# The residual x1 + b3 made in the base stage of a two-layer LoRA, convolution and gated-FFN kernel, with the convolution's last loads reordered

## The reference, cut to what matters

```python
# x: (32, 64, 1024) = 2048 rows of 1024
x = x + L0_ffn(L0_cond(x, cond))     # = x1
x = x + L1_ffn(L1_cond(x1, cond))    # = x1 + silu-gated FFN of the convolved x1

# L0_cond: a 64x64 channel mix per batch (a mixture of 8), plus a bias           -> y
# L0_ffn:  y @ kernel + bias + LoRA of the group's own adapter and a shared one
# L1_cond: grouped 1-d convolution of x1 with 9 taps, plus a context and a bias   -> c
# L1_ffn:
x12 = einsum('bsk,mk->bsm', c, w12) + b12
x1_, x2_ = split(x12, 2)
return einsum('bsm,nm->bsn', silu(x1_) * x2_, w3) + b3
# and the last line of the whole: out = x1 + (... @ w3.T + b3)
```

## Time and profile before

| | us |
|---|---|
| median of 3 runs | 844.76 |
| lowest, highest | 843.33, 848.78 |
| the profiled execution | 842.09 |
| its span, first to last instruction | 840.3 |
| TensorE busy | 819.3 (98%) |
| DVE busy | 384.4 (46%) |
| ACT busy | 150.0 (18%) |
| POOL busy | 84.6 (10%) |

### The profile page before, as it was taken

How to read it: one execution, slowest core, us unless ns; L and a number is a source line. 1 busy time by engine, 2 the same in 40 slices (tenths; PEclk the granted TensorE clock), 3 DMA queues, 4 the chain that set the end, 5 groups by cost and what they waited for, 6 DMA issues and landing times.

```text
span 840.3 us, 10782 instructions
## 1 busy us (share of the span) xinstructions
PE 819.3 (98%) x4081; PEld 691.8 (82%) x4081; DVE 384.4 (46%) x456; ACT 150.0 (18%) x194; POOL 84.6 (10%) x59
## 2 busy tenths in 40 slices
PE   5998999999999999999999999999999989999998
PEld 4876888888888999888888888888888868888886
DVE  4864442414230787525343433121243975655552
ACT  3431110101000334201120112010102432111110
POOL 4440433231321000000000000000000000000000
PEclk9999999999999999999999999999999999999999
DMA  8946853643639872335353533020334244444441
GB/s 249 284 127 207 217 143 92 154 122 112 164 86 238 215 171 62 116 135 166 126 168 121 170 131 100 25 75 25 104 96 112 87 163 151 150 151 150 164 161 75
DMA packets 72873, 116.89 MB, mean 139 GB/s; under 512 B 10680, under 2 KB 50024, under 8 KB 72840
## 3 DMA queue, kind: packets, MB, share of 16 engines
q1 hardware_dynamic: 69632, 115.35, 46.4%
q10 hardware_dynamic: 3064, 0.90, 0.6%
q0 software_dynamic: 144, 0.21, 0.1%
HBM read 70.92 MB, written 44.45 MB: 137 GB/s over the span
## 4 chain that ended last, share of the span: by engine, by line
PE 89%; DVE 4%; DMA 3%; issue 1%; SPq 1%; ACTq 1%; ACT 0%; DVEq 0%
PE ps L1285 72%; PE ps L1546 17%; DVE w_t_f L1086 1%; DMA lb<-lb_c_lo 1%; DMA raw<-in_L_ffn_w 1%; DMA h_f<-h_scratch 1%; ACTq L323 1%; DVE w_t_lo L1091 1%; SPq L465 1%; DVE h_s L1133 0%; DMA gate_t<-in_L_ffn_gate 0%; PE ps L1330 0%; DVE w_n L1080 0%; DVE lb_c_lo L991 0%; DVE hs_lo L1203 0%
## 5 line engine op out<-in xcount | busy, mean ns | idle before, releaser
L1285 PE MATMUL ps<-c_hi,w_hi 128*128 128x512 f32 x512 | 199.3, 389 | 0.0
L1285 PE MATMUL ps<-c_hi,w_lo 128*128 128x512 f32 x512 | 199.2, 389 | 0.0
L1285 PE MATMUL ps<-c_lo,w_hi 128*128 128x512 f32 x512 | 199.2, 389 | 0.0
L1133 DVE SCALAR_TENSOR_TENSOR h_s<-ps,b_s,silu_s 128x512 f32<-128x512 f32 x32 | 24.0, 751 | 195.9 <-PE ps L1285 195.6
L1285 PEld LDWEIGHTS ps<-c_hi,w_hi 128*128 128x128 f32 x512 | 96.1, 188 | 20.1
L1285 PEld LDWEIGHTS ps<-c_lo,w_hi 128*128 128x128 f32 x512 | 96.1, 188 | 19.9
L1285 PEld LDWEIGHTS ps<-c_hi,w_lo 128*128 128x128 f32 x512 | 96.1, 188 | 19.8
L1285 PE MATMUL ps<-wk_hi,y_hi 128*128 128x512 f32 x256 | 80.5, 395 | 0.4 <-issue 0.4
L1285 PE MATMUL ps<-wk_lo,y_hi 128*128 128x512 f32 x256 | 79.1, 390 | 0.0
L1285 PE MATMUL ps<-wk_hi,y_lo 128*128 128x512 f32 x256 | 78.9, 389 | 0.0
L979 DVE TENSOR_TENSOR x_t<-ps,x_t 128x1024 f32<-128x1024 f32 x16 | 19.6, 1225 | 122.2 <-PE ps L1285 118.0
(11 more groups left out here) (156 smaller groups left out, 961.1 us busy)
## 6 DMA issues: line engine op xcount, KB each, us to landing
raw<-in_L_ffn_w SPq DMA_DIRECT2D x96, 128.0 KB, 3.1
x_scratch<-x_t SPq DMA_DIRECT2D x16, 516.0 KB, 2.7
x_scratch<-x_t SPq DMA_DIRECT2D x128, 64.5 KB, 2.4
x<-x_scratch SPq DMA_DIRECT2D x32, 258.0 KB, 6.1
x_in<-x_scratch SPq DMA_DIRECT2D x16, 516.0 KB, 4.1
x_in<-in_x SPq DMA_DIRECT2D x16, 512.0 KB, 4.5
h_scratch<-h_s SPq DMA_DIRECT2D x32, 256.0 KB, 2.2
r_scratch<-r_t SPq DMA_DIRECT2D x16, 512.0 KB, 2.9
```

Of the source, the lines that this page charges most:

```text
L1133: dve.scalar_tensor_tensor(out=h_s[rb][:, :], in0=bank(2 * rb + 1), scalar=b12_s[:, 1, ds(j, 1)], in1=silu_s[rb % 2][:, :], op0=ALU.add, o ...
L1285: return pe.matmul(o, l, r, start=start, stop=stop)
```

## The change

The rows of x1 are no longer stored to DRAM and loaded back. DVE makes r from the tile `x1_t` in the base stage, directly behind take_x1, into one of two buffers `r_t` that lie where raw[0] and raw[1] lie, and SP stores it behind the eight x8 stores of the tile. `b3_s` moves to raw[2]'s place and is loaded in the setup. As the buffers of w12 are now taken by r_t until the last r store, `load_w12(0)` moves behind these stores; slices 4 and 5 of the convolution are loaded ahead of that wait. The gate stage loses the residuals and is written as a loop on DVE.

```diff
-    x1_dram = nc.dram_tensor("x1_scratch", [ROWS, PH * (BLK + 1)], F32).ap()
...
-        x1_in = at("x1_in", [P, 2, HB + 1], 182.25)
-        r_t = at("r_t", [P, NL], 186.3125)
-        b3_s = at("b3_s", [P, NL], 190.3125)
+        r_t = [at(f"r_t{s}", [P, NL], 199.75 + 4 * s) for s in range(2)]
+        b3_s = at("b3_s", [P, NL], 90)
...
             load_wk(6)
             load_wk(7)
+            wait_slot(sp, raw_of(5))
+            sp.dma_start(b3_s[:, :], b3.partition_broadcast(P)).then_inc(b3_in, 16)
             sp.wait_ge(lbs_made, 2)
...
             def store_x1(t, s, made):
                 sp.wait_ge(x1_made, made)
                 sp.wait_ge(pads_made, 4)
-                sp.dma_start(x1_dram[ds(t * P, P), :], slots(x1_t[s])).then_inc(x1_stored[s], 16)
                 for n in range(2 * GRP):
                     sp.dma_start(x8_rows[n, ds(t, 1)].rearrange("a c k e -> (a c) k e"),
                                  slots(x1_t[s])[n * CG:(n + 1) * CG, :].rearrange("p (k e) -> p k e", e=BLK + 1)
                                  ).then_inc(x1_stored[s], 16)
+                sp.wait_ge(r_made, made - 2)
+                sp.dma_start(r_dram[ds(t * P, P), :], r_t[s][:, :]).then_inc(r_stored[s], 16)
...
             load_c_bias(0)
-            load_w12(0)
             sp.wait_ge(y_mm, 2 * TILES)
             sp.wait_ge(xb_made, TILES)
             for s in range(2):
-                sp.wait_ge(x1_stored[s], 144 * 2)
+                sp.wait_ge(x1_stored[s], 128 * 2)
             for t in range(4):
                 load_x8(t)
             store_x1(TILES - 2, 0, TILES + 1)
             store_x1(TILES - 1, 1, TILES + 2)
             load_c_bias(1)
             for s in range(2):
-                sp.wait_ge(x1_stored[s], 144 * TILES // 2)
-            for t in range(4, TILES):
+                sp.wait_ge(x1_stored[s], 128 * TILES // 2)
+            load_x8(4)
+            load_x8(5)
+            for s in range(2):
+                sp.wait_ge(r_stored[s], 16 * TILES // 2)
+            load_w12(0)
+            for t in range(6, TILES):
                 load_x8(t)
...
-            sp.wait_ge(conv_mm, NB)
-            sp.dma_start(b3_s[:, :], b3.partition_broadcast(P)).then_inc(b3_in, 16)
-            sp.wait_ge(c_taken, NB + 8)
-            with sp.Fori(0, 4) as j:
-                load_w12(j + 1)
-                for rb in range(RB):
-                    load_x1(j * 4 + rb)
-                    store_h(j, rb)
-                    store_r(j * 4 + rb)
-            with sp.Fori(4, NJ - 2) as j:
+            with sp.Fori(0, NJ - 2) as j:
                 load_w12(j + 1)
                 for rb in range(RB):
                     store_h(j, rb)
...
-            sp.wait_ge(r_stored, 16 * TILES)
...
-                    pool.wait_ge(x1_stored[k % 2], i * 288 + 144 * (k // 2 + 1))
+                    pool.wait_ge(x1_stored[k % 2], i * 256 + 128 * (k // 2 + 1))
+                    pool.wait_ge(r_made, i * 4 + k + 1)
...
+            def residual(t, s, free):
+                dve.wait_ge(x1_made, t + 3)
+                if free is not None:
+                    dve.wait_ge(r_stored[s], free)
+                dve.tensor_tensor(r_t[s][:, :].rearrange("p (b h q) -> p h q b", h=2, q=4), blocks(x1_t[s]),
+                                  b3_s[:, :].rearrange("p (b h q) -> p h q b", h=2, q=4), ALU.add).then_inc(r_made, 1)
+
+            dve.wait_ge(b3_in, 16)
+            for pair in range(2):
+                dve.wait_ge(lb_stored[pair], 64)
+            dve.wait_ge(lb_loaded[0], LB_FIRST[0])
+            residual(0, 0, None)
+            residual(1, 1, None)
+
             def take_group(i, k):
                 t, g = i * 4 + 2 * k, i * 2 + k
                 take_y(t + 2, 1 - k, 0)
                 take_x1(t, 0)
+                residual(t, 0, i * 32 + 16 * k)
                 take_y(t + 3, 1 - k, 1)
                 take_x1(t + 1, 1)
+                residual(t + 1, 1, i * 32 + 16 * k)
                 take_z(g + 1, 1 - k)
...
-            def gate_steps(i, with_residual):
+            def gate_steps(i):
...
-            gate_steps(0, True)
-            gate_steps(1, True)
-            gate_steps(2, False)
-            dve.wait_ge(r_stored, 16 * TILES)
+            gate_steps(0)
+            with dve.Fori(1, 3) as i:
+                gate_steps(i)
```

More of the change, by code:

```diff
@@ L262, in layered_kernel @@
         h_loaded = [sem(f"h_loaded{s}") for s in range(2)]
-        x1_loaded, r_made, r_stored = sem("x1_loaded"), sem("r_made"), sem("r_stored")
+        r_made, r_stored = sem("r_made"), [sem(f"r_stored{s}") for s in range(2)]
         w3_hi_made, w3_lo_made, w3_sum_made = sem("w3_hi_made"), sem("w3_lo_made"), sem("w3_sum_made")
@@ L519, in store_h @@
                              h_s[rb][:, :]).then_inc(h_stored[rb], 16)
-            def load_x1(t):
-                sp.wait_ge(r_made, t + 1)
-                sp.dma_start(slots(x1_in), x1_dram[ds(t * P, P), :]).then_inc(x1_loaded, 16)
-            def store_r(t):
-                sp.wait_ge(r_made, t + 2)
-                sp.dma_start(r_dram[ds(t * P, P), :], r_t[:, :]).then_inc(r_stored, 16)
-            sp.wait_ge(conv_mm, NB)
-            sp.dma_start(b3_s[:, :], b3.partition_broadcast(P)).then_inc(b3_in, 16)
-            sp.wait_ge(c_taken, NB + 8)
-            with sp.Fori(0, 4) as j:
-                load_w12(j + 1)
-                for rb in range(RB):
-                    load_x1(j * 4 + rb)
-                    store_h(j, rb)
-                    store_r(j * 4 + rb)
-            with sp.Fori(4, NJ - 2) as j:
+            with sp.Fori(0, NJ - 2) as j:
                 load_w12(j + 1)
@@ L673, in _ @@
             for t in range(TILES - 4, TILES - 2):
-                pool.wait_ge(x1_stored[t % 2], 144 * (t // 2 + 1))
+                pool.wait_ge(x1_stored[t % 2], 128 * (t // 2 + 1))
+                pool.wait_ge(r_made, t + 1)
                 pool.wait_ge(x_loaded[(t + 2) % 4], 16 * ((t + 2) // 4 + 1))
@@ L881, in _ @@
             dve.sem_inc(h_made, 4)
-            dve.sem_inc(r_made, 1)
             dve.wait_ge(consts_made, 2)
@@ L1049, in _ @@
             take_x1(12, 0)
+            residual(12, 0, 96)
             take_y(15, 1, 1)
             take_x1(13, 1)
+            residual(13, 1, 96)
             take_z(7, 1)
             take_x1(14, 0)
+            residual(14, 0, 112)
             take_x1(15, 1)
+            residual(15, 1, 112)
             def turn(n_in, s, value, half, n_free):
@@ L1137, in _ @@
             dve.wait_ge(c_lo_made, NB + 4)
-            def residual(j, rb):
-                dve.wait_ge(x1_loaded, (j * 4 + rb) * 16 + 16)
-                if not (isinstance(j, int) and j == 0 and rb == 0):
-                    dve.wait_ge(r_stored, (j * 4 + rb) * 16)
-                dve.tensor_tensor(r_t[:, :].rearrange("p (b h q) -> p h q b", h=2, q=4), blocks(x1_in),
-                                  b3_s[:, :].rearrange("p (b h q) -> p h q b", h=2, q=4), ALU.add).then_inc(r_made, 1)
-            def gate_steps(i, with_residual):
+            def gate_steps(i):
                 for k in range(2):
@@ L1150, in gate_steps @@
                     turn_w12(j + 1)
-                    if with_residual:
-                        residual(j, 0)
                     hidden(j, 1)
                     w12_lo_part(j + 1, 1 - k)
-                    if with_residual:
-                        residual(j, 1)
-                    for rb in range(2, RB):
-                        hidden(j, rb)
-                        if with_residual:
-                            residual(j, rb)
-            dve.wait_ge(b3_in, 16)
-            gate_steps(0, True)
-            gate_steps(1, True)
-            gate_steps(2, False)
-            dve.wait_ge(r_stored, 16 * TILES)
+                    hidden(j, 2)
+                    hidden(j, 3)
+            gate_steps(0)
+            with dve.Fori(1, 3) as i:
+                gate_steps(i)
             hidden(6, 0)
```

2 lines of the change are left out of this document (1 added, 1 removed).

## The result

The changed kernel took 850.22 us (median of 20 runs, 843.29 to 854.62) beside 844.94 us for the kernel before on the same chip (20 runs): ratio 1.005, 95% interval 1.0029 to 1.007. The forecast was 846.0 us with a range of 842.0 to 851.5. So the time lies in the range and within 1% of the forecast, but the forecast's +1.2 us were +5.3 us, and no step of the sum comes to that.

A forecast was written before the change was run, and what follows sets the result against it. The prediction took TensorE, busy 98% of the span, as the bound. Its terms 0 + 0 + 0.5 + 0.7 = +1.2 us on 844.76 gave 846.0 us, with an 8-in-10 range of 842.0 to 851.5.

The forecast's parts named there:

- the forecast's +1.2 us: Whole kernel: sum of 0 + 0 + 0.5 + 0.7 us, added to 844.76 to give 846.0 us.
- What bounds the kernel: From 69 to 640 us TensorE waits once, 3.8 us; only what delays TensorE counts.
- Part 1: Gate stage: residual additions, x1 loads and r stores leave a stage where TensorE never waits; worth 0.
- Part 2: Base stage: residual added behind take_x1; tightest at z_group(2), margin 0.8 us, cost 0, bounds 0 to 1.4 us.
- DVE late at z_group(2), 1.4 us at most: Rival in the base stage's first group: TensorE waits for DVE, at most 1.4 us, 847.4 us; chance 0.04.
- Wrong: a wait of TensorE at z_group(2): Sign against the forecast: TensorE waiting at z_group(2) or any later group in the base stage.
- Part 3: SP's setup queue: early b3 load delays y_bias about 4.7 us, to 52.5; cost 0.5 us, bounds 0 to 2.2.
- The +0.5 us: Setup term: y_bias' data overlapping the critical LoRA copies on the DMA engines, taken near the low end.
- Part 4: Base-to-convolution seam: w12(0) and r store ahead of x8(6) make TensorE wait 0.7 us, bounds 0 to 2.0.
- x8(4): 286.0 + 0.8 = 286.8 against 287.2, no wait: Convolution start: x8(4), 0.8 us later for the r store, still lands before TensorE needs it.
- The rival with the fallen clock: Seam: TensorE waits 2.0 us, then a slowed clock costs 1.6 more, 848.9 us; chance 0.11.
- y_bias ahead of the copies: Setup rival: y_bias goes out just before the sixteen critical copies, 2.2 us instead of 0.5, 847.7 us; chance 0.08.

The follow-up runs named there:

- after_again: The changed kernel, unchanged, run once more as yardstick for the other runs; 851.63 us, 1.0068 against the kernel before.
- b3_behind: The changed kernel with b3's load and its wait moved behind the six shared LoRA copies, ahead of the x tiles; 853.07 us, 1.0092.
- slices_first: The changed kernel with x8(6) to x8(8) loaded ahead of the wait for the r stores and of w12(0); 851.39 us, 1.0049.
- seam_alone: The changed kernel with last r store, second c_bias and w12(0) behind x8 loads at the seam, DVE order unchanged; 850.64 us, 1.007.
- y_first: The changed kernel with take_y of the second tile and take_z ahead of the residuals on DVE, all groups; 849.14 us, 1.0047.
- y_setup: The changed kernel with y_first's DVE order, b3 behind the shared copies, x tile 5 behind group 1's LoRA loads; 847.73 us, 1.0018.
- before_again: The kernel before, unchanged, one execution for a second profile; 847.92 us.
- before_add: The kernel before plus one unused DVE addition with two SBUF inputs behind take_x1(2) in the first group; 847.59 us, 1.0016.
- before_b3: The kernel before with the changed kernel's early b3 load and its wait, into a tile nobody reads; 848.43 us, 1.0029.
- all_moves: The changed kernel with y_first's DVE order, b3 behind the shared copies, x tile 5 behind group 1's LoRA loads, and a reordered seam; 845.82 us, 1.0002.
- y_seam: The changed kernel with y_first's DVE order and all_moves' seam, b3 and x tile 5 left in the changed kernel's places; 845.23 us, 0.9996.

## Why the forecast was too low

**The account that the table gives.** z_group(2): the five profiles with after's order on DVE (after, after_again, b3_behind, slices_first, seam_alone) lose 0, 4.1, 5.4, 6.2 and 6.0 us against 171.11 in the base groups, a mean of 4.3 us; the eight with another order and no added addition lose 0.0. The seam: the five with after's seam (after, after_again, b3_behind, y_first, y_setup) take 411.76 to 415.41 us for convolution and gate, mean 412.75; the four profiles with before's seam (before, before_again, before_add, before_b3) 410.10 to 412.39, mean 410.8: 2.0 us. Together 6.3 us, from single executions, beside +5.3 and +6.4 us between the medians. Setup and first group: u_lora(3) starts at 104.1 on average in the five profiles made from before and at 103.5 in the nine made from after. The end stage is 158.8 and 158.7 us. In these means those two hold nothing.

The medians, which come from far more executions, say the same if all nine results of kernels made from after are taken together. Five have after's order on DVE (mean ratio 1.0066), four the other (1.0016): 0.50%, 4.2 us. With the order the same, after's seam against the mended one is 1.0070 against 1.0060, and 1.0033 against 0.9999: 0.22% on average, 1.9 us. By the runs' intervals each of the two is good to about 0.16%.

**What bounds the kernel.** Right, and it is the part that held best: what left the gate stage bought nothing (Part 1). all_moves and y_seam have the waits of the change at z_group(2) and at the seam mended and all of its relief, and they stand at before's time, not below it; their convolution and gate take 409.99 and 410.06 us, before's 410.10.

**Part 2 failed, and it is the largest term: "Margin 0.8 us, cost 0" and "the residual's own 2.2 us bounds it, 0 to 1.4 us".** The order was worked out rightly and the durations were taken as fixed. The residual has two inputs in SBUF, and GpSimd's x_plus_bias runs just there: 2.2 us became 4.55, and the residual pushed the y_lo pair, 1.29 us, behind the next x_plus_bias, where it became 4.95. So the bound was not 2.2 us but 2.2 + 2.4 + 3.7 = 8.3, of which 1.8 to 3.7 reached TensorE as a wait. The rival "DVE late at z_group(2), 1.4 us at most" had the right place and a chance of 0.04. The clue stood in the trace of before. Between the rows lies the y_lo pair of take_y(5), with 2.41 us and not 1.29, beside GpSimd's additions until 97.63 (97.63 + 1.29 = 98.9, and the pair ended at 98.78). DVE's timeline of before:

```profile
96.37 2.41 DVE L954 TENSOR_TENSOR y_lo<-y_f,y_hi 128x512 fp32r<-128x512 f32 x2 [0.16 <-ACT y_hi L723]
```

The prediction took its end from the row after it and never asked why it was so long. y_first takes the residual away from there and before_add puts an addition there, and the wait goes and comes with it; the prediction's own test, "Wrong: a wait of TensorE at z_group(2)", is met in after_again and three more, though not in the first profile of after. What the prediction also lacks is the full price of a wait: 1.84 us of waiting made the stage 3.6 us longer, 2.62 us 4.1, 2.99 us 6.0, 3.65 us 6.2, 3.68 us 5.4. The rest goes with the clock of 0.50 behind it: at 0.50 from 107.24 to past 112, seam_alone does some 5.5 us of work at half the rate, by estimate 2.7 us of loss, where 3.0 were lost beside the wait. The prediction applied this only to the seam.

**Part 3: the moves as forecast, the price not found.** y_bias was issued at 53.58 (forecast 52.5) and first_group_lb at 57.20, but in an execution in which everything was late by some 2.5 us already. That lag was there before y_bias: the first product lb_t,gate_e began at 48.71 in after and at 46.20 in before. The +0.5 us are not seen: y_seam with the early b3 load is at 0.9996, all_moves without it at 1.0002, and b3_behind is no faster than after_again. For a price speak before_b3 (1.0029, that is 0.8 to 4.1 us), whose profile doesn't show where, and the step from y_first to y_setup, which moves b3 and x tile 5 (1.0047 to 1.0018, with about 0.27% of noise). Whether there is one stays open. What Part 3 did miss is a cliff: group 1's LoRA loads landed 0.2 us ahead of their use in the trace of before (issued at 80.77 with 4.5 us to land, used at 85.50), and in after TensorE waited 3.1 us for them. It is a shared bill, though: where the wait for lb_c_lo is 3.7 us or more this second one is 0 to 0.4, and where it is 2.2 to 3.2 us, it is 1.2 to 3.1. It comes with TensorE being early, and u_lora(3) starts at 103.9 on average in the five profiles with 1.2 us or more of it and at 103.6 in the other nine.

**Part 4: right mechanism, two terms too small.** "295.1 against 294.4: TensorE waits 0.7 us" measured, in the same five profiles, 1.36, 1.7, 1.8 (two waits), 1.7 (two waits) and 3.3 us (two waits), and 2.0 us in the stretch's mean. The mis-sized term is what lies ahead of x8(6): its last half needed 8.70 us to land and was in place 23.1 us after the start of the convolution (277.67), forecast 22.2. And "x8(4): 286.0 + 0.8 = 286.8 against 287.2, no wait" did not hold in b3_behind, slices_first, y_first and y_setup, where TensorE waited 0.3 to 0.9 us for x8(4). The r store ahead of it was taken as +0.8 us with a bound of 2.1; no run parts it from scatter, as before_again waited 1.8 us for x8(4) without it. The rival with the fallen clock was seen once, in y_setup (+5.4 us on 410.0); in after and y_first the clock stayed at 1.00 behind a wait of 1.4 us.

**The range.** Its upper end, 851.5, was made of y_bias ahead of the copies and of the seam with a fallen clock. The largest loss was neither, so that 850.22 lies inside is luck.

**What isn't settled.** The traces say that DVE's order is worth 4.3 us, the medians of all nine 4.2. Single pairs scatter about that. Between y_seam and seam_alone it is 0.74% (6.2 us), but between y_first and after it is 0.03%, against after_again 0.21%, each ± about 0.3%. Against the sum of two separate terms y_first is too slow and after too fast, each by about its own interval. One term of 4 us or so seen with this scatter is the likeliest reading; that the two edits need each other is not excluded, and no run here tells these apart.

## What to carry to other kernels

A duration read from the trace is good only beside the same neighbours: before an operation with two SBUF inputs is put on DVE, look at which GpSimd instructions run there, and look in the trace of before for the same DVE operation with a longer time than it mostly takes. An added operation belongs behind whatever the bottleneck's next input is, even when the margin looks positive. And before one profile's gap is explained, split a second execution of both kernels by the same marks: of the 8.1 us between the two profiles here, 3.4 us lay in a stretch in which the next execution had no such wait.
